# A first attention stage: cubic with a double root, and the f16 planes made by ScalarE and VectorE

## The reference

```
importance, alpha = sigmoid(x @ Wimp.T), sigmoid(x @ Walpha.T)      # per row; per row and head
q, k, v = x @ Wqkv.T + bqkv
euclid  = q @ k.T / 4
q_hyp, k_hyp = expmap0(q / |q| * s), expmap0(k / |k| * s)
inner   = -q_hyp[0] k_hyp[0] + sum(q_hyp[1:] k_hyp[1:])
hyper   = -arccosh(max(-inner, 1 + 1e-6))**2 / curv[h]
scores  = (1 - alpha) * euclid + alpha * hyper, causal
y       = softmax(scores) * (importance > threshold) @ v ; then y @ Wout.T
```

## Time and profile before

| | us |
|---|---|
| median of 3 runs | 2325.63 (2318.34 to 2330.01) |
| the profiled execution | 2335.74, its span 2333.9 |
| first attention, first to last big Square of ACT | 105.8 to 1013.9 |

### The profile page before, as it was taken

How to read it: one execution, slowest core, us unless ns; L and a number is a source line. 1 busy time by engine, 2 the same in 40 slices (tenths; PEclk the granted TensorE clock), 3 DMA queues, 4 the chain that set the end, 5 groups by cost and what they waited for, 6 DMA issues and landing times. The chain is left out here.

```text
span 2333.9 us, 39090 instructions
## 1 busy us (share of the span) xinstructions
PE 1863.9 (80%) x12343; PEld 1136.9 (49%) x12344; DVE 1617.1 (69%) x3456; ACT 1476.8 (63%) x2762; POOL 613.7 (26%) x638
## 2 busy tenths in 40 slices
PE   3678787878887877766998988898873799999990
PEld 1345454545554554442333333333233688888880
DVE  3488888898989897855766667666726455555556
ACT  1388989889898989961566666665651333333333
POOL 4331414151505050014102212220111233333320
PEclk9688999999899989987999999998975899999995
DMA  1221212121212121102101133443436411111116
GB/s 41 68 62 44 68 42 67 38 70 40 68 42 67 43 62 39 37 11 80 47 25 55 51 92 123 145 132 119 128 100 266 149 45 45 45 45 45 45 41 220
DMA packets 143652, 172.38 MB, mean 74 GB/s; under 512 B 27457, under 2 KB 123922, under 8 KB 141458
## 3 DMA queue, kind: packets, MB, share of 16 engines
q1 hardware_dynamic: 135010, 149.59, 21.0%
q0 software_dynamic: 7488, 20.46, 2.9%
q10 hardware_dynamic: 1008, 0.54, 0.1%
HBM read 105.47 MB, written 65.01 MB: 73 GB/s over the span
## 5 line engine op out<-in xcount | busy, mean ns | idle before, releaser
L1270 DVE TENSOR_REDUCE NM<-sP 128x1 f32<-128x512 f32 x512 | 332.6, 684 | 182.0 <-PE sP L1148 179.0
L1080 ACT ACTIVATE PT<-tP 128x512 f32<-128x512 f32 x512 | 285.8, 603 | 213.0 <-PE tP L1159 212.1
L478 ACT ACTIVATE YZ<-YZ,gsc 128x512 f32<-128x512 f32 (+3 forms) x512 | 344.1, 711 | 56.3 <-DVE YZ L665 56.1
L1516 ACT ACTIVATE H<-hP,B1T 128x256 f32<-128x256 f32 x312 | 127.3, 473 | 273.2 <-PE hP L1595 201.2
L676 DVE CUSTOM_DVE_ANT_0 YZ<-SeP,YZ 128x512 f32<-128x512 f32 (+3 forms) x512 | 239.9, 485 | 36.7 <-PE SeP L543 30.9
L542 PE MATMUL SeP<-SMV,SST 128*128 128x512 f16 (+3 forms) x512 | 162.3, 322 | 126.2 <-DVE mn L676 124.6
L665 DVE SCALAR_TENSOR_TENSOR YZ<-YZ,XL 128x1280 f32<-128x1280 f32 x128 | 200.3, 1565 | 54.9 <-ACT YZ L470 53.9
L456 ACT ACTIVATE XL<-mP 128x512 f32<-128x512 f32 (+1 forms) x384 | 221.2, 577 | 20.6 <-PE mP L553 19.2
L464 ACT ACTIVATE PTa<-tPa 128x512 f32<-128x512 f32 (+1 forms) x384 | 224.3, 584 | 12.1 <-PE tPa L574 11.5
L1148 PE MATMUL sP<-STK,STQ 112*128 112x512 f16 x512 | 205.4, 403 | 29.1 <-DVE NM L1270 20.0
L568 PE MATMUL tPa<-ident,YZ 128*128 128x128 f32 x1280 | 219.4, 289 | 1.5 <-DVE DG L683 0.7
(11 more groups left out here) (305 smaller groups left out, 4124.2 us busy)
## 6 DMA issues: line engine op xcount, KB each, us to landing
X<-in_L_ffn_W SPq DMA_DIRECT2D x32, 512.0 KB, 4.3
weight_planes<-X SPq DMA_DIRECT2D x64, 256.0 KB, 2.4
SST<-planes_a_scratch SPq DMA_DIRECT2D x384, 32.0 KB, 1.8
SMV<-planes_a_scratch SPq DMA_DIRECT2D x384, 32.0 KB, 1.8
planes_a_scratch<-HI SPq DMA_DIRECT2D x64, 128.0 KB, 1.7
planes_a_scratch<-LO SPq DMA_DIRECT2D x64, 128.0 KB, 1.8
Y<-results_scratch SPq DMA_DIRECT2D x16, 512.0 KB, 8.7
STQ<-planes_scratch SPq DMA_DIRECT2D x96, 64.0 KB, 2.6
```

What stands on the lines that cost most here:

```text
L478: act.activation(w, w, ACT.Square, bias=gsc[:, b % 2, 1, i, hh:hh + 1], scale=gsc[:, b % 2, 0, i, hh:hh + 1]).then_inc(hyp_ready, 1)
L1080: act.activation(PT[:, p % 4, par, kt, :], tP[x % 3][:, :], ACT.Exp).then_inc(exp_done, 1)
L1270: dve.tensor_reduce(NM[:, g % 2, col:col + 1], sP[n % 2][:, :], AX.X, ALU.max, negate=True).then_inc(max_done, 1)
```

## The change

The fit is written with a double root: with L = ln(...) the cubic is (L + a)^2 (L + b). ACT's Ln yields L + b by its gain (LOG_SHIFT), ACT's Square takes the bias a - b from the column `shiftr`, and DVE's product is max(Square, SQUARE_FLOOR) * XL, so that the clamp lies within it. The scaled Square is then Square(gain * YZ) with no base. The clamp, its semaphore and half of gsc with its instruction are gone. ACT's Square of head s stands at step (s, 3), DVE's product of head s-1 at (s, 2); NXL is 2 and NYZ 6. For the planes ACT copies `mis` straight to HI as f16, waiting for the stored buffer; DVE, one step later, writes LO = mis - HI and releases the bank; SP waits for that. QF is gone, and POOL has no part in it.

```
-LOG_OFFSET = 0.92431640625
-LOG_GAIN = 0.0015895932404133247
-CUBIC_LIN = -410.5611091772769
-CUBIC_GAIN = -0.0022214880475452344
-CUBIC_BASE = 7.643709854001822
-LOG_FLOOR = log(LOG_GAIN * (1.0 + 1e-6 + LOG_OFFSET))
+LOG_OFFSET = 0.8916015625
+LOG_SHIFT = -31.3262757157778
+LOG_GAIN = exp(LOG_SHIFT)
+ROOT_SHIFT = 5.930873622256664
+ROOT_GAIN = -0.0019921336708390485
+SQUARE_FLOOR = (log(1.0 + 1e-6 + LOG_OFFSET) + ROOT_SHIFT) ** 2
...
-            NXL = 3
-            NYZ = 5
+            NXL = 2
+            NYZ = 6
...
+                    chain(dve.memset(shiftr[:, :], ROOT_SHIFT - LOG_SHIFT))
...  SP
-                            sp.wait_ge(lo_ready, u + 1)
+                            sp.wait_ge(pb_out, nth[kind, i, b] + 1)
...  POOL
-                        for kind, i, b in pieces(n, 2, "keh"):
-                            u = units[kind, i, b]
-                            pool.wait_ge(pb_out, nth[kind, i, b] + 1)
-                            if u >= 2:
-                                pool.wait_ge(pl_stored[u % 2], 32 * (u // 2))
-                            pool.tensor_copy(HI[:, u % 2, :], QF[:, u % 2, :]).then_inc(hi_ready, 1)
-                            pool.wait_ge(hi_ready, u + 1)
-                            pool.tensor_tensor(LO[:, u % 2, :], QF[:, u % 2, :], HI[:, u % 2, :], ALU.subtract).then_inc(lo_ready, 1)
...  ACT
-                        h = s - 1
-                        if t == 2 and 0 <= h < HEADS:
-                            act.wait_ge(clamped, h + 1)
-                            if h >= NYZ:
-                                act.wait_ge(tp_full, 3 * (h - NYZ + 1))
-                            act.activation(YZ[:, h % NYZ, :], XL[:, h % NXL, :], ACT.Square).then_inc(y_ready, 1)
...
-                            act.activation(w, w, ACT.Square, bias=gsc[:, b % 2, 1, i, hh:hh + 1],
-                                           scale=gsc[:, b % 2, 0, i, hh:hh + 1]).then_inc(hyp_ready, 1)
+                            act.activation(w, w, ACT.Square, scale=gsc[:, b % 2, i, hh:hh + 1]).then_inc(hyp_ready, 1)
+                        if t == 3 and 0 <= s < HEADS:
+                            act.wait_ge(ln_ready, 3 * (s + 1))
+                            if s >= NYZ:
+                                act.wait_ge(tp_full, 3 * (s - NYZ + 1))
+                            act.activation(YZ[:, s % NYZ, :], XL[:, s % NXL, :], ACT.Square, bias=shiftr[:, :]).then_inc(y_ready, 1)
...
-                                    act.wait_ge(lo_ready, u - 1)
-                                act.activation(QF[:, u % 2, :], mis[:, :], ACT.Copy).then_inc(pb_out, 1)
+                                    act.wait_ge(pl_stored[u % 2], 32 * (u // 2))
+                                act.activation(HI[:, u % 2, :], mis[:, :], ACT.Copy).then_inc(hi_ready, 1)
...  DVE
-                        h = s - 2
-                        if t == 0 and 0 <= h < HEADS:
-                            dve.wait_ge(y_ready, h + 1)
-                            dve.scalar_tensor_tensor(YZ[:, h % NYZ, :], YZ[:, h % NYZ, :], CUBIC_LIN, XL[:, h % NXL, :],
-                                                     ALU.add, ALU.mult).then_inc(z_ready, 1)
...
                         h = s - 1
-                        if t == 1 and 0 <= h < HEADS:
-                            dve.wait_ge(ln_ready, 3 * (h + 1))
-                            w = XL[:, h % NXL, :]
-                            dve.tensor_scalar(w, w, LOG_FLOOR, None, ALU.max).then_inc(clamped, 1)
+                        if t == 2 and 0 <= h < HEADS:
+                            dve.wait_ge(y_ready, h + 1)
+                            dve.scalar_tensor_tensor(YZ[:, h % NYZ, :], YZ[:, h % NYZ, :], SQUARE_FLOOR, XL[:, h % NXL, :],
+                                                     ALU.max, ALU.mult).then_inc(z_ready, 1)
...
+                        for kind, i, b in pieces(n, 2, "keh"):
+                            u = units[kind, i, b]
+                            if u >= 2:
+                                dve.wait_ge(pl_stored[u % 2], 32 * (u // 2))
+                            dve.wait_ge(hi_ready, u + 1)
+                            dve.tensor_tensor(LO[:, u % 2, :], mis[:, :], HI[:, u % 2, :], ALU.subtract).then_inc(pb_out, 1)
...
-                            chain(dve.tensor_scalar(gsc[:, b % 2, 0, :, :], root[:, :, 4 * H:5 * H], CUBIC_GAIN, None, ALU.mult))
-                            chain(dve.tensor_scalar(gsc[:, b % 2, 1, :, :], root[:, :, 4 * H:5 * H], CUBIC_BASE, None, ALU.mult))
+                            chain(dve.tensor_scalar(gsc[:, b % 2, :, :], root[:, :, 4 * H:5 * H], ROOT_GAIN, None, ALU.mult))
```

More of the change, by code:

```diff
@@ L12 @@
 from contextlib import ExitStack
-from math import factorial, log
+from math import exp, factorial, log
 import concourse.bass as bass
@@ L128, in build @@
             root = stat
-            gsc = sb(ctx, "gsc", [P, 2, 2, NT, H])
+            gsc = sb(ctx, "gsc", [P, 2, NT, H])
+            shiftr = sb(ctx, "shiftr", [P, 1])
             spk = sb(ctx, "spk", [P, 3, NT])
-            QF = sb(ctx, "QFa", [P, 2, T])
             HI = sb(ctx, "HI", [P, 2, T], F16)
@@ L287, in build @@
             hi_ready = sem("hi_ready")
-            lo_ready = sem("lo_ready")
             pl_stored = [sem(f"pl_stored_a{i}") for i in range(2)]
@@ L292, in build @@
             ln_ready = sem("ln_ready")
-            clamped = sem("clamped")
             y_ready = sem("y_ready")
```

## The result

The changed kernel takes 2306.75 us (median of 9 runs, 2295.43 to 2310.3) against 2325.63 of the kernel before (9 runs beside it, 2318.34 to 2333.29): a ratio of 0.9911 [0.989, 0.9933], 19 us faster where 65 were forecast. The direction was right and the size was not: 2306.75 lies outside the range of 2240 to 2291.

A forecast was written before the change was run, and what follows sets the result against it. The first attention was held bound by ACT and DVE nearly equally, plus 11.6 us per batch of waits. Six batches gain 52, the first 7, the last 6: 65 us, so 2261 us on the median, range 2240 to 2291.

The forecast's parts named there:

- The base pointer: ACT's Squares in the first attention: 0.10 us per pointer, 0.30 per head, 4.8 per batch saved.
- the nine heads: ACT-bound part of a steady batch: ACT 55.0 us plus 1.2 idle, 56.2 in all, a gain of 3.2.
- The clamp into the product: DVE: the clamp goes, the product keeps its length; 0.87 us per head, 14 per batch less work.
- The wait loop cut open: ACT's wait for DVE's product before the scaled Square: the 8.1 us per batch should go nearly whole.
- HI by ACT, LO by DVE: Planes: ACT's copy unchanged at 0.48 us; DVE's subtract 0.684, or 0.61 without overlap, 4.9 per batch.
- POOL's relief: POOL loses HI and LO, so DVE's two-input instructions stretch less: 3.2 us per batch, bounds 1 and 5.
- The three heads: Part of a batch with DVE's chain of small statistics: from 30.40 to 27.0 us, a gain of 3.4.
- rival 4: Better than forecast: clock near 1 in the chain's heads, idle time there and in projections vanishes; 2238 us, chance 0.15.
- The piece chain: PE's next piece waits for DVE's subtract: hidden in ACT-bound heads, 1.2 us idle kept; 5.6 per batch if uncovered.
- Rival 3: Slower than before: subtract behind the product, PE stalls, clock drops, 2 us per unit; 2377 us, chance 0.03.
- 2: PE and the piece chain become the bound, gain about half: 2293 us; chance 0.22 together with the free-pointer rival.
- The first batch: First batch of 16 heads in the first attention, 105.6 us with the same pieces: a gain of 7.

The follow-up runs named there:

- g: The changed kernel with a column of zeros as bias pointer of the four scaled Squares again: 2324.99 us, ratio 0.9965.
- c: The changed kernel with DVE's product moved from the head to the end of its sub-step: 2287.56 us, ratio 0.9833.
- d: The changed kernel with the bank released by ACT's copy; DVE's LO instruction reads zeros in SBUF, low plane left out: 2280.45 us, ratio 0.9795.
- a: The changed kernel with its planes part undone: ACT copies to QF and releases the bank, POOL makes HI and LO: 2289.32 us, ratio 0.9833.
- h: Kernel a (planes by ACT's f32 copy and POOL) with DVE's product put last in its sub-step: 2290.47 us, ratio 0.9819.
- e: The changed kernel with product last, ACT copying to QF and releasing the bank, DVE making HI and LO from QF: 2283.43 us, ratio 0.9777.
- k: Kernel f with POOL's four adds to XR held until the last h unit has left the bank: 2271.38 us, ratio 0.9753.
- l: Kernel k with the two small DVE copies before the first h unit one sub-step earlier: 2271.08 us, ratio 0.9746.
- b: The kernel before with the planes part alone, HI by ACT and LO by DVE out of the bank: 2340.91 us, ratio 1.0053.
- f: Kernel e with DVE's reads of the bank (QK, AI, VSa, Y) moved to the head of the sub-step: 2267.89 us, ratio 0.9711.

## Why the prediction was right in sign and wrong in size

**The base pointer: right**, 0.092 for 0.10, and a saturated head at 5.50 for 5.52. What it is worth in this kernel was overrated: three pointers net were counted in full, 4.8 us per batch and 34 in all. The four of g should then cost 0.37 x 128 = 47 us, and cost 13 to 18; the nine heads, which wait for PE, feel 0.2 us of them in the batch shown.

**The clamp into the product: right.** The product kept its length (1.524 mean, 1.580 in the earlier trace rows). DVE's 90.4 us per batch stand against 92.6 by the prediction's terms (105.1 less 14, 3.2 and 0.2, plus 4.9), ACT's 102.4 against 101.5, PE's 94.9 against 95.5.

**The wait loop cut open: right**, the 8.1 us per batch of the scaled Square are 0. Ln's wait for the product with two XL buffers, priced at 0, is 0.3 per batch in the change. It becomes 2 to 5 as soon as the product is put last.

**HI by ACT, LO by DVE: prices right**, LO 0.688 us for 0.684.

**POOL's relief: right in kind.** L779, now L769, from 1247 to 281 ns; DG from 858 to 744. The groups by form, DVE, 210 to 800:

```profile
L667 DVE TENSOR_TENSOR DG<-identh,mn 128x512 f16<-128x512 f16 x81 | 60.3, 744 | 3.0 <-DVE mn L660 0.2
...
L692 DVE TENSOR_TENSOR LO<-misc,HI 128x512 f16<-128x512 f32 x40 | 27.5, 688 | 10.4 <-ACT HI L486 10.4
...
L769 DVE TENSOR_TENSOR stat<-st 128x128 f32<-128x128 f32 x5 | 1.4, 281 | 0.0
```

The three heads came out at 26.84 for 27.0 in the batch shown, with the clock up from 0.78 to 0.87. That batch flatters: over six batches they take 27.8 on average, and the clock is 0.72 to 0.87 where it was 0.77 to 0.91. So the clock did not rise, and rival 4, which needed it near 1, failed.

**The piece chain: wrong, and this is the step that failed.** "ACT may be two steps behind PE, about 3 us, and piece plus mP take about 1.7, so in ACT-bound heads it is hidden", and "I keep 1.2 us of idle time in the nine heads for it". Measured there: ACT is busy 55.68 as forecast (55.0), and idle 7.5 us instead of 1.2. Three errors are in that step.

1. The cover was reckoned as if ACT lagged PE by two steps, about 3 us. No row stood behind that lag; the timeline now shows ACT idle 2.54 us behind a piece that is 2.64 us late, so nearly nothing was covered.
2. The price was one subtract and its semaphore, 0.7 us. The waits are up to 2.6 us each, since what delays the reader is the queue ahead of it. PE's waits for LO alone are 8.0 us per batch, and all its waits for DVE 13.1, where the upper bound was 5.6.
3. The product's move was checked against its waits and its readers, and not against what it now stands ahead of. Rival 3 had exactly that ("DVE's subtract stands behind the 1.4 us product") with a chance of 0.03, for the subtract only and with the product's own place taken as given. Kernel c shows that this order is worth 18 us, and d that the longer hold of the bank is worth 27; a, which gives the planes back to POOL as well, is worth 18. As either remedy shortens the batch by 3 to 4 us and h, with both, by no more, the two overlap: largely one stall, which grows past its cover by both, and not two that add.

Of the rivals, 2 named the mechanism (PE and the bank that passes through two engines) and gave 2293; the measured time is 14 us further on that side. Against it I held that "the window of nine heads has 11 us of PE idle". That idle is no reserve: the stall comes in single lumps of 2 to 3 us and mP is behind them in program order. The prediction itself had this among the signs that it is wrong: "if PE waits for DVE's subtract before each piece with ACT waiting for mP behind it".

The size follows: the six batches take 116.3 us each where 109.2 were forecast, 43 of the 46 us that are missing, and 6.5 of these 7.1 us lie in the nine heads. The first batch gained 6.7 us (2nd to 18th big Square) where 7 were forecast, the last 4.3 where 6 were. The prediction's rows for both cover 15 heads and not 16, since the big Square at 105.8 is the second of the stage (the first is at 100.85); nothing in the result hangs on it.

Even without that stall the forecast was too low. The best nine heads of the table (58.7) have ACT busy 55.1 and idle 3.6 with PE's clock at 0.97. So about 2.5 of the 7.0 us are a term that none of the remedies gave back. What bounds them there, the minimum that PE's SeP waits for, mP or Ln's wait for the product, stays open: taking away one wait at a time (e, k, l) moved the batch by less than 1 us. A third XL buffer beside six YZ, which would have told the product's part, was not tried. Nor was the move of the big Square to its own head taken back by itself.

## What to carry to other kernels

Before an instruction is moved in a queue that runs in program order, list what comes to stand behind it, and who waits for that; its own producer and consumer are the smaller half of the question. For a buffer that many steps share, add up from full to free the work of every engine in the chain and the queue ahead of each: giving the last read to another engine can lengthen the hold by the queue of that engine, whatever the sums of busy time say. Idle time of an engine in a window is not cover by itself: here stalls of 2 to 3 us went through to ACT while PE had 12 us of idle time in the window. So look at the longest single wait, and not only at the sum, and try the two halves of a change alone: here one half was slower than nothing.

## What the runs showed of the hardware

A DVE instruction of 128x64 f32 with one input from SBUF, 0.22 us otherwise, took 2.51 us beside POOL's adds of 2.76 us in SBUF, and went on until shortly after the last of them had ended (585.65). It looks as if it stood still for all of POOL's run; in five instances the mean was 2057 ns, and 218 with the adds elsewhere. This is a far larger factor than the 1.25 for 0.29 us of the earlier trace rows, and on an instruction with one SBUF input. The Trainium skill, GPSIMD Engine Reference, Specifications, names a two-port mode of VectorE beside two SBUF inputs as what collides; whether this instruction ran in that mode no row here shows.

PE's SeP matmul of 512 columns in f16 took 0.63 us behind a wait of 2.64 us (at 606.82) and 0.38 us at 612.51. The table of windows for these two stretches:

```profile
605.94:608.90 2.96, 2.96 (x12) 2.25 (x13) 1.55 (x6) 0.60 (x1) 0.00 (x0) 0.50 0.02 6
...
612.30:614.50 2.20, 2.20 (x21) 1.08 (x19) 2.17 (x5) 2.20 (x6) 0.00 (x0) 1.00 0.49 148
```

The granted clock was 0.50, the lower of its two levels (1.2 GHz), right behind the wait, and 1.00 (2.4 GHz) 6 us later; in the wait itself, 603.30 to 605.90, it was 0.98. So this stall of PE was paid twice, by the wait itself and by slow work behind it: 51.2 us busy in the nine heads at a clock of 0.92, against 48.3 for the same work at 0.97 in c. But the low clock does not go with PE's waits for DVE alone. Kernel h has as few of them as e, and its nine heads, in the batch shown in the table of kernels, were

```profile
697.36:757.77 60.41, 51.28 (x362) 33.71 (x363) 43.64 (x115) 55.57 (x110) 17.72 (x17) 0.92 0.19 56
```

while b, with its waits for LO, was at 0.97 in three of six batches. In f, batches of one kernel go from 57.4 us at 1.00 to 59.3 at 0.91. What lowers the clock in h, and how much of the nine heads' length the clock makes rather than follows, is not shown.
